# Projection by PSUM bank, softmax by bank, and transposes of P and V moved from TensorE to the DMA crossbar

## What is computed

```python
def _L0_attn_ref(x, Wkqv, bkqv, Wp, bp):          # x already layer-normed
    y = jnp.einsum('bnd,hde->bhne', x, Wkqv) + bkqv[None, :, None, :]
    k, q, v = y[..., :Dm], y[..., Dm:2 * Dm], y[..., 2 * Dm:]   # 1024, 1024, 64
    A = jnp.einsum('bhnd,bhmd->bhnm', q, k) / jnp.sqrt(jnp.float32(Dm))
    A = jnp.where(causal_mask, A, -jnp.inf)
    A = jax.nn.softmax(A, axis=-1)
    sa = jnp.einsum('bhnm,bhmd->bnhd', A, v).reshape(Bm, Nm, Dm)
    return sa @ Wp + bp
```

## Time and profile before

| | us |
|---|---|
| median of 3 runs (lowest, highest) | 9792.33 (9750.43, 9816.27) |
| the profiled execution | 9700.75 |
| its span on core 3, the slowest | 9698.9 |
| spans, cores 0 to 3 | 9686.0, 9689.0, 9692.5, 9698.9 |
| spans, cores 4 to 7 | 9644.6, 9660.5, 9663.1, 9649.0 |
| mean granted clock, cores 0 to 3 and 4 to 7 (medians) | 0.746, 0.755 |
| busy on core 3: TensorE, VectorE, ScalarE, GpSimd | 5941.6, 1792.1, 1114.7, 175.8 |

### The profile page before, as it was taken

One profiled execution on the slowest core, in us unless ns is written; L12 is line 12 of the kernel. 1 busy time (PEld: TensorE's weight loads), 2 busy tenths in 40 slices (PEclk: granted clock), 3 DMA queues, 4 the chain that ended last, 5 costly groups with the idle time before them and its releaser, 6 DMA issues.

```text
span 9698.9 us, 65305 instructions; the slowest of 8 cores (9644.6 to 9698.9 us)
## 1 busy us (share of the span) xinstructions
PE 5941.6 (61%) x24192; PEld 2603.0 (27%) x24192; DVE 1792.1 (18%) x3242; ACT 1114.7 (11%) x1868; POOL 175.8 (2%) x231
## 2 busy tenths in 40 slices
PE   4456536666665666666566666656666665455546
PEld 1122212322222222222222222222322222122212
DVE  2212201212112121211212121121212112112211
ACT  1111101010101101010110101011010101111101
POOL 0000000000000000000000000000000000000000
PEclk8666767777777777777777777777777777677777
DMA  3221131000000100000010000001000000421222
GB/s 66 44 44 24 37 55 18 5 14 9 10 13 5 18 5 14 9 10 13 5 18 5 14 9 10 13 5 18 5 14 9 10 0 1 129 34 39 41 51 37
DMA packets 170404, 213.64 MB, mean 22 GB/s; under 512 B 20816, under 2 KB 154224, under 8 KB 167792
## 3 DMA queue, kind: packets, MB, share of 16 engines
q0 software_dynamic: 154192, 155.24, 10.9%
q1 hardware_dynamic: 15904, 54.25, 1.6%
HBM read 339.49 MB, written 25.17 MB: 38 GB/s over the span
## 4 chain that ended last, share of the span: by engine, by line
PE 59%; DVE 16%; DMA 9%; ACT 8%; issue 6%; DVEq 1%; ACTq 0%; POOLq 0%; SPq 0%
PE psF L646 25%; PE psF L727 14%; PE psF L415 7%; PE psF L379 5%; DVE Kb L659 4%; ACT Qb L670 4%; ACT Pst L767 3%; DMA f2a<-f 3%; DMA f2b<-f 3%; PE psF L823 3%; DVE stat L751 3%; DVE PTs L807 2%; PE psT L802 2%; DVE Pst L793 1%; PE psF L336 1%
## 5 line engine op out<-in xcount | busy, mean ns | idle before, releaser
L646 PE MATMUL psF<-ln_fm,wsl 128*128 128x512 bf16 x8704 | 2436.0, 450 | 941.0 <-DVE Kb L659 470.5
L646 PEld LDWEIGHTS psF<-ln_fm,wsl 128*128 128x128 bf16 x8704 | 963.5, 113 | 2408.7 <-issue 1745.6
L727 PE MATMUL psF<-Kb,Qb 128*128 128x512 bf16 (+3 forms) x5120 | 1383.6, 445 | 0.0
L802 PE MATMUL psT<-ident,Pst 128*128 128x128 bf16 x2176 | 292.3, 297 | 1218.1 <-DVE Pst L793 1176.5
L727 PEld LDWEIGHTS psF<-Kb,Qb 128*128 128x128 bf16 x5120 | 581.0, 121 | 722.7 <-issue 465.2
L670 ACT ACTIVATE Qb<-psF,bkqvq_sb 128x512 bf16<-128x512 f32 x512 | 351.7, 687 | 2715.2 <-PE psF L646 2679.1
L659 DVE TENSOR_SCALAR Kb<-psF,bkqv_sb 128x512 bf16<-128x512 f32 x512 | 384.5, 751 | 1328.8 <-PE psF L646 1285.9
L415 PE MATMUL psF<-mha,f2a 128*128 128x512 bf16 x1024 | 353.4, 523 | 342.9 <-DMA f2a<-f 334.9
L802 PEld LDWEIGHTS psT<-ident,Pst 128*128 128x128 bf16 x2176 | 194.4, 128 | 1374.8 <-issue 1374.8
L415 PE MATMUL psF<-mhb,f2b 128*128 128x512 bf16 x1024 | 346.7, 515 | 325.7 <-DMA f2b<-f 317.8
L767 ACT ACTIVATE Pst<-psF,stat 128x1536 bf16<-128x1536 f32 (+13 forms) x288 | 307.1, 1066 | 2040.6 <-DVE stat L751 1695.9
(11 more groups left out here) (107 smaller groups left out, 2209.9 us busy)
## 6 DMA issues: line engine op xcount, KB each, us to landing
wsl<-wkqv POOLq DMA_DIRECT2D x64, 1024.0 KB, 9.6
f2a<-f POOLq DMA_DIRECT2D x64, 512.0 KB, 5.4
f2b<-f POOLq DMA_DIRECT2D x64, 512.0 KB, 5.3
f1a<-f POOLq DMA_DIRECT2D x8, 1024.0 KB, 9.5
xta<-x SPq DMA_DIRECT2D x4, 2048.0 KB, 8.4
xs<-xta SPq DMA_DIRECT2D x4, 2048.0 KB, 7.1
x1t<-xs SPq DMA_DIRECT2D x4, 2048.0 KB, 8.0
xs<-x1t SPq DMA_DIRECT2D x4, 2048.0 KB, 7.9
```

The costliest lines, as they stand in the source:

```text
L646: outap=outap, ts=ts: e.matmul(outap, wsl[g][:, gw * c + 128 * jj: gw * c + 128 * jj + ofw], ln2_fm[:, 2048 * c + 512 * ts: 2048 * c + 512 ...
L727: lambda e, c=c, i=i, kw=kw, st=st, qb=qb: e.matmul(bank(st[i], kw), Qb[:, 2048 * c + 128 * qb: 2048 * c + 128 * (qb + 1)], Kb[:, 2048 * c ...
L802: (lambda e, col, i2=4 * tg + q, par=par: e.transpose(psT[:, col: col + 128], Pst[par][:, 128 * i2: 128 * (i2 + 1)], ident[:]))
```

## The change

- Projection: the loop over ts is now outside that over c. Each bank gets its 8 matmuls in a row, waits only for its own earlier copy, raises sT by itself, and is copied out at once.
- V: the 16 TensorE transposes and 4 copies of a head give way to one DMA transpose issued from SyncE, of all 128 partitions of `Vfm` (the upper 64 are set to zero once), into a `Vtm` twice as wide. The copies into `Vfm` now also wait for sIO.
- Softmax: maximum and exponential go bank by bank (nb pieces instead of one or two), with a join of the maxima and a join of the sums for every qb.
- P: the qb+1 TensorE transposes of a block with their copies give way to one DMA transpose from SyncE. It waits for the scaled P, for the V matmuls of the block before, and for all earlier DMAs on sIO; the V matmuls wait for it.

```diff
-            Vtm = p2.enter_context(nc.sbuf_tensor("Vtm", [128, 1024], BF16))
+            Vtm = p2.enter_context(nc.sbuf_tensor("Vtm", [128, 2048], BF16))
...
+            sch.emit("vector", lambda e: e.memset(Vfm[64:128, :], 0.0),
+                     waits=list(entry2), inc="sV")
...
-                        w = [("sW", wdone[g])]
                         for ts in range(4):
-                            w += [("sS", bankS[ts]), ("sV", bankV[ts])]
+                            w = [("sW", wdone[g]),
+                                 ("sS", bankS[ts]), ("sV", bankV[ts])]
+                            if h == 0 and j == 0 and ts == 0:
+                                w += entry2
                             if j > 0:
                                 w.append(ev[(j - 1, ts)])
-                        if h == 0 and j == 0:
-                            w += entry2
-                        for c in range(8):
-                            for ts in range(4):
-                                outap = (bank(ts) if ofw == 128
-                                         else psF[0:64, 512 * ts: 512 * ts + 512])
+                            outap = (bank(ts) if ofw == 128
+                                     else psF[0:64, 512 * ts: 512 * ts + 512])
+                            for c in range(8):
                                 sch.emit("tensor",
                                          lambda e, g=g, gw=gw, c=c, jj=jj, ofw=ofw,
                                          outap=outap, ts=ts: e.matmul(
...
-                                         waits=w if (c == 0 and ts == 0) else [],
-                                         inc="sT" if (c == 7 and ts == 3) else None)
-                        mmj = sch.cnt["sT"]
-                        for ts in range(4):
+                                         waits=w if c == 0 else [],
+                                         inc="sT" if c == 7 else None)
...
-                                         waits=[("sT", mmj), ("sV", v_init)],
+                                         waits=[("sT", mmj), ("sV", v_init),
+                                                ("sIO", vt_io_prev[0])],
                                          inc="sV")
...
-                for vg in range(4):
-                    tiles = [
-                        (lambda e, col, i2=4 * vg + q: e.transpose(
-                            psT[:, col: col + 128],
-                            Vfm[:, 128 * i2: 128 * (i2 + 1)], ident[:]))
-                        for q in range(4)]
-                    psT_group(tiles,
-                              lambda e, col, vg=vg: e.tensor_copy(
-                                  Vtm[:, 256 * vg: 256 * (vg + 1)].rearrange(
-                                      "p (s v) -> p s v", s=4),
-                                  psT[:, col: col + 512].rearrange(
-                                      "p (s v) -> p s v", s=4)[:, :, 0:64]),
-                              waits_extra=[("sV", vfm_done),
-                                           ("sT", av_done.get((h - 1, 15), 0))])
-                vtm_done = sch.cnt["sV"]
+                sch.emit("sync", lambda e: e.dma_start_transpose(
+                    Vtm[:].rearrange("p (i q) -> p i q", i=16),
+                    Vfm[:].rearrange("p (i k) -> p i k", i=16)),
+                    waits=[("sV", vfm_done), ("sT", av_done.get((h - 1, 15), 0)),
+                           ("sIO", sch.cnt["sIO"])],
+                    inc="sIO", inc_amt=16)
+                vtm_done_io = sch.cnt["sIO"]
+                vt_io_prev[0] = vtm_done_io
...
-                    if par == 0:
-                        pieces = [(0, 0, W)]
-                    else:
-                        pieces = [(0, 1536, min(W, 1536))]
-                        if W > 1536:
-                            pieces.append((1536, 0, W - 1536))
-                    npc = len(pieces)
-                    if npc == 1:
-                        sch.emit("vector", lambda e, pc=pieces[0], par=par: e.reduce_max(
-                            stat[:, 26 + par: 27 + par],
-                            psF[:, pc[1]: pc[1] + pc[2]], AX, negate=True), inc="sV")
-                    else:
-                        for idx, pc in enumerate(pieces):
-                            sch.emit("vector", lambda e, pc=pc, idx=idx: e.reduce_max(
-                                stat[:, 20 + idx: 21 + idx],
-                                psF[:, pc[1]: pc[1] + pc[2]], AX), inc="sV")
-                        sch.emit("vector", lambda e, par=par, npc=npc: e.reduce_max(
-                            stat[:, 26 + par: 27 + par], stat[:, 20: 20 + npc], AX,
-                            negate=True), inc="sV")
+                    for i in range(nb):
+                        kw = min(512, W - 512 * i)
+                        sch.emit("vector", lambda e, i=i, kw=kw, st=st: e.reduce_max(
+                            stat[:, 20 + i: 21 + i], bank(st[i], kw), AX),
+                            waits=[("sV", sch.cnt["sV"])] if i == 0 else [],
+                            inc="sV" if i == nb - 1 else None)
+                    sch.emit("vector", lambda e, nb=nb, par=par: e.reduce_max(
+                        stat[:, 26 + par: 27 + par], stat[:, 20: 20 + nb], AX,
+                        negate=True),
+                        waits=[("sV", sch.cnt["sV"])], inc="sV")
                     mxd = sch.cnt["sV"]
-                    for idx, pc in enumerate(pieces):
-                        acc = (smx[:, 8 + 2 * par: 9 + 2 * par] if npc == 1
-                               else smx[:, 4 * par + idx: 4 * par + idx + 1])
+                    order = [3, 0, 1, 2] if nb == 4 else list(range(nb))
+                    for i in order:
+                        kw = min(512, W - 512 * i)
                         sch.emit("scalar",
-                                 lambda e, pc=pc, par=par, acc=acc: e.activation(
-                                     Pst[par][:, pc[0]: pc[0] + pc[2]],
-                                     psF[:, pc[1]: pc[1] + pc[2]], AF.Exp,
+                                 lambda e, i=i, kw=kw, st=st, par=par: e.activation(
+                                     Pst[par][:, 512 * i: 512 * i + kw],
+                                     bank(st[i], kw), AF.Exp,
                                      bias=stat[:, 26 + par: 27 + par],
-                                     accum_out=acc),
+                                     accum_out=smx[:, 4 * par + i: 4 * par + i + 1]),
                                  waits=[("sV", mxd),
-                                        ("sT", tr_done.get((h, qb - 2), 0))],
+                                        ("sIO", tr_done.get((h, qb - 2), 0))],
                                  inc="sS")
-                        mkpc = sch.cnt["sS"]
-                        for i in range(nb):
-                            cb = 512 * st[i]
-                            if pc[1] <= cb < pc[1] + pc[2]:
-                                exp_piece[(h, qb, i)] = mkpc
-                                bankS[st[i]] = mkpc
+                        exp_piece[(h, qb, i)] = sch.cnt["sS"]
+                        bankS[st[i]] = sch.cnt["sS"]
                     expall = sch.cnt["sS"]
-                    if npc > 1:
-                        sch.emit("vector", lambda e, npc=npc, par=par: e.reduce_sum(
-                            smx[:, 8 + 2 * par: 9 + 2 * par],
-                            smx[:, 4 * par: 4 * par + npc], AX),
-                            waits=[("sS", expall)], inc="sV")
+                    sch.emit("vector", lambda e, nb=nb, par=par: e.reduce_sum(
+                        smx[:, 8 + 2 * par: 9 + 2 * par],
+                        smx[:, 4 * par: 4 * par + nb], AX),
+                        waits=[("sS", expall)], inc="sV")
                     ls_mark = sch.cnt["sV"]
...
-                    for tg in range((ntile + 3) // 4):
-                        cnt4 = min(4, ntile - 4 * tg)
-                        tiles = [
-                            (lambda e, col, i2=4 * tg + q, par=par: e.transpose(
-                                psT[:, col: col + 128],
-                                Pst[par][:, 128 * i2: 128 * (i2 + 1)], ident[:]))
-                            for q in range(cnt4)]
-                        psT_group(tiles,
-                                  lambda e, col, tg=tg, cnt4=cnt4: e.tensor_copy(
-                                      PTs[:, 512 * tg: 512 * tg + 128 * cnt4],
-                                      psT[:, col: col + 128 * cnt4]),
-                                  waits_extra=[("sV", nrm),
-                                               ("sT", av_done.get(
-                                                   (h, qb - 1),
-                                                   av_done.get((h - 1, 15), 0)))])
-                    tr_done[(h, qb)] = sch.cnt["sT"]
-                    ptv = sch.cnt["sV"]
+                    sch.emit("sync", lambda e, par=par, ntile=ntile: e.dma_start_transpose(
```

(25 more changed lines are left out.)

## The result

| | before | after |
|---|---|---|
| median of the runs, us | 9772.21 (10 runs, 9662.9 to 9989.15) | 9221.14 (9 runs, 8851.36 to 9450.74) |
| span of the profiled execution, slowest core | 9698.9 | 8853.6 |
| ratio | | 0.9139, 95% interval 0.9081 to 0.9197 |

The ratio 0.9139 of 9792 is 8949 us.

A forecast was written before the change was run, and what follows sets the result against it. Attention was taken as a serial chain on TensorE, its projection idle for copies. Projection -1340, scores +144, softmax +365, transposes -554 and +1018, V +64 sum to -303 us: 9792 to 9490 us, range 9050 to 10800.

The forecast's parts named there:

- What bounds the kernel: Attention heads fill 6.8 of 9.7 ms: a chain without overlap, plus projection idle time of 941.0 us, nearly all for copies.
- The copies cost nothing beside the matmuls: Projection: copies of 0.83 us each run beside the next banks' matmuls and cost nothing; chance of the opposite 0.02.
- The clock of the projection: Three eighths of the projections were taken at clock 0.81, so the gain was 1340 us instead of 1490 at full clock.
- Scores, 9 us a head more: Attention scores would run more at 1.2 GHz as TensorE stands still before them: 144 us in all, bounds 0 and 480.
- A further block at 0.25 us: DMA transpose of P: each 128x128 block after the first costs 0.25 us; transposes of P 1018 us in all.
- The fixed part, 2.1: DMA transpose of P: the first block of each DMA takes 2.1 us, 16 DMAs a head.
- V, where 64 were forecast: DMA transpose of V: 4 us a head stand out beyond block 0's scores and softmax, 64 us in all.
- Softmax by bank: Extra pieces of maximum and exponential and extra joins stand on the path: 22.7 us a head, 365 us in all.
- The crossing paid packet by packet: Rival: a further DMA transpose block costs 0.6 to 0.9 us; at 0.88 the kernel takes 10830 us; chance 0.24.
- The rival of the clock: Rival: all dense projections run at 0.81, costing 250 us, so 9740 us and no change; chance 0.15.
- The low bound: Sum with full clock throughout, the low bound of the transposes and unchanged scores: 8929 us, partly left out of the range.

The follow-up runs named there:

- e1: The kernel before with only the projection's new bank order, TensorE transposes and one- or two-piece softmax kept: span 8156.1 us, ratio to before 0.8402.
- e2: The changed kernel with the softmax put back to one or two pieces: span 8492.9 us, ratio to before 0.8786.
- e3: The changed kernel with the transposes of P and V put back on TensorE: span 8553.9 us.
- e5: The changed kernel with every DMA transpose of P made 16 blocks wide, the extra blocks unread: span 9143.0 us.
- e4: The changed kernel with matmuls nobody reads added between each block's scores and its V matmuls: span 8490.1 us.

## Why the prediction was right in sign and wrong in size

- **What bounds the kernel: right.** Attention is a chain; e1, e2 and e3 give the same sum by terms as the traces, and the wait for the four copies was all of the projection's idle time but for the 42.9 us of the first load.
- **The copies cost nothing beside the matmuls: right.** L648 has no idle time but the load.
- **The clock of the projection: the step that failed first.** "I take three eighths of them at 0.81" took 150 us off the gain. None was at 0.81: at the forecast's 0.262 us a matmul a head takes 142.5 us, and 1920.0 / 16 is 120.0; the other cores whose 8704 matmuls are all in the trace have 1905 to 1918 us. At full clock the forecast's own figure, 1490, is the measured 1491. The three eighths were counted in the wrong place. They come from feed-forward stretches of two cores of one die; the same view of core 5, on the other die, has its eight stretches at 0.97 to 1.00. And the projection's own steps could be asked: on core 3, where three feed-forward stretches had 0.81, the step shown above ends at 1.00, and so do all 263 steps that the timeline of the kernel before shows whole (the 2 us that end 0.5 us before each step's end). On core 0, 3 of 92 had 0.81.
- **Scores, 9 us a head more: wrong.** The argument named TensorE's transposes as what kept its clock up. But the rows it cited, a burst of 2.1 us at full clock that took 4.45, already said that bursts start at 1.2 GHz with those transposes in place, and the window above has 0.50 there. Nothing was left to lose; the lower bound, 0, was the value. This is 169 us, with the 25 that the scores fell.
- **A further block at 0.25 us: mis-sized.** It measured 0.145 (e5), below even the row of 0.17. The 0.08 that I put on top for the scattering of the pieces had no row. This is 202 us. The fixed part, 2.1, was 2.2 in the same count (2.45 from the end of the scaling, less the 0.25 that TensorE's transposes too wait from there in e3's timeline), 26 us the other way; 895 - 16 x 16 x 2.2 - 1920 x 0.145 leaves 54 for V, where 64 were forecast. The 54 is what is left over and was not measured by itself.
- **Softmax by bank: right**, 383 against 365. (22.7 x 16 is 363, and the 214.4 us of a projection come to 214.3 by their rows; neither matters.)
- **The rivals.** The crossing paid packet by packet, to which I gave 0.24, is refuted in its price, 0.88 us a block. Its picture of 8 packets on each of 16 engines was right in the count, and that they largely follow one another is not excluded; what was wrong is the 0.110 us of a packet, taken from q0, where the packets are of about 1 KB and come from weight loads. Those of the transpose took some 0.023 (the estimate above). The rival of the clock did not come: the projections had the full clock.
- **The low bound: luck in part.** The sum of low bounds, 8929, "which I leave partly out" of the range, is what came, within 20 us. Clock and scores did lie at their cheap end. But the transposes of P came to 841 us and not 784, V to 54 and not 32, the softmax to 383 and not 365; these 97 us are made up by the 25 of the scores and by 53 outside attention, of which 35 are chance.

What stays open: why the projections get the full clock while feed-forward stretches of the kernel before got 0.81 on cores of one die. No run here was made for it. In the changed kernel's profile all eight cores are in the projection at once, 1393 to 1510 us, with granted clocks of 0.95 to 1.00. The Trainium skill (TensorE: Matmul & The Clock Gate, Part 1) gives 13/16 of the clock, 0.81, once three cores of a die run dense matmuls; the profiled execution does not show it in its projections.

## What to carry to other kernels

Let each PSUM bank be finished, signalled and copied by itself: the loop order alone was worth about 1500 us here, and it is seen in the profile as an idle time before every group of matmuls that equals the copies, followed by matmuls at half the clock. In a serial chain a transpose costs its whole latency wherever it runs; by DMA it took about 2.2 us plus 0.145 us a further 128x128 block here, and it paid, by 1%, only once the next block's work was issued beside it. When a cost is bounded from below by a row, take the row; a margin on top needs a row of its own, and the clock of a stretch is read from that stretch, on cores of both dies, and not borrowed from other code.

## What the runs showed of the hardware

- Adding 8800 matmuls of no use made a kernel 364 us faster (8853.6 to 8490.1), since without them TensorE falls to 1.2 GHz in the pauses of the softmax (0.50 in the window shown); the slices of the granted clock over the span (tenths of full speed) show it, first the changed kernel, then e4:

```profile
PEclk9787677687786877868778676877868777777777
```

```profile
PEclk9677677999999999999999999999999997777777
```

- In six kernels (before, changed, e1, e2, e3, e5) the time of the scores stayed within 25 us while the wait beside it ranged from 1730 to 2732 us: the longer pauses cost no more clock, and short transposes on TensorE within them gave none back.
- A DMA transpose kept SyncE's queue for 1.56 us at 14 blocks, and the wait for it grew by 0.145 us a block, 227 GB/s.
